# A channel mix placed behind the context's keys and values in the first attention unit of a fused RWKV and attention kernel

## The chip, the cores and the metric

The program runs on one core of one Trainium2 chip. The metric is the device time of one execution in microseconds (us), lower is better. The five engines used are TensorE (matmul), VectorE, ScalarE, GpSimd and SyncE, which here only issues DMA transfers.

## The reference, cut to what matters

Four layers run one after another on x (16 sequences of 128 tokens, 256 channels), all in float32: an RWKV mixer with a channel mix (L0), a cross-attention to a context (L1), a second RWKV mixer with channel mix (L2), a second cross-attention with an MLP (L3).

```python
x = _L0_xattn_ref(x, ctx_2048, ...)          # time mix, recurrence over the tokens, then channel mix
x = _L1_xattn_ref(x, ctx_2048, mask, ...)    # a = layer_norm(ctx); Q from x, K and V from a; x + tanh(gate) * out
x = _L2_xattn_ref(x, ctx_2048, 0, ...)
x = _L3_xattn_ref(x, ctx_2048, mask, ...)
```

What matters here: the K and V of L1 come from the layer norm of the context alone, and need nothing of x. The channel mix of L0 needs the x that the recurrence of L0 ends with:

```python
xc = _ln(x, ln2_w, ln2_b)                # channel mix
rr = sigmoid(xr2 @ fWr.T); kk = square(relu(xk2 @ fWk.T))
x = x + rr * (kk @ fWv.T)
```

## The kernel before, in words

The 16 sequences are worked on in four groups of four; 128 tokens lie on the partitions, or, after a transpose, 128 channels. For each layer pair and group there are two units: a *mixer* and an *attention unit*. STEPS lists eight of each (layers L0 and L1 of groups 0 to 3, then L2 and L3), four MLP units follow. The program of a mixer is written as two generators, `head` (H: norm, low-rank parts, projections of W, K, V, R, G) and `recurrence` (R: scans, outer products, the y sums, the output projection, x update). The channel mix of L0 is part of the attention unit of L1 (`attn`, A), since in the chain of units it comes just ahead of it; its semaphores have the prefix `f`.

Each engine runs its instructions strictly in the order in which they were emitted, and the order is written out by hand. A generator stops at each `yield`; the stretch between two yields is a step. ORDER (L103) has one string per engine, and `in_order` (L134) takes for each letter the next step of H, R or A:

```python
for letter in ORDER[engine]:
    next(programs[letter], None)
```

So a step can stand behind another one that waits on a semaphore, and is then held up by it, whatever its own inputs. VectorE has 595 such steps, ScalarE 540, TensorE 828, GpSimd 48.

The steps that the text speaks of, by their lines:

- Head, VectorE: five low-rank parts (`mix_low_rank`, L442), each a product in PSUM (L449) and a sum (L458), then the gate (L545). The parts make the inputs of W, K, V, R and G, in this order. TensorE: low-rank matmuls (L1184, the last ones L1198), w1 (L1223, L1228), projections of K, V and R (L1267), of G (L1281). ScalarE copies K, V, R out of PSUM (L892).
- Recurrence, VectorE: outer products (`outer`, L473), the reduction into RU (L556), for each of four chunks c two scans (L563) and a product with R_ (L571). An outer product for c of 2 or more waits until TensorE has summed the y of chunk c-2 (L1301). GpSimd makes YT = R * K * u (L780, L781), which the reduction into RU reads, and V * RU (L786). TensorE adds that in at L1291 and projects the output at L1129. VectorE adds it to x (L605).
- Attention unit of L1, in the emitted order of before: the bias split (L623, L626, first unit only); the channel mix: norm of x (L413, L421), transposes (L1079), shift (L439), two mixes (L432), key projection (L1088), two token projections (L1129), x update (L498, L499); then the norm of the context (mask work L636 to L641, L413, L421 into az), transposes of x (L1079 into QA) and of az (L1079 into QB), the Q projection (L1088 into QA), the K projection (L1088 into QB), the V projection (L1129 into QA); copies by ScalarE (L946, L993, L958, L975); then 16 score jobs.
- A norm takes VectorE's statistics, then GpSimd's power -0.5 (`inv_std`, L765: L767 and L768), then VectorE's application.
- A score job is a mask matmul (L1375) and two matmuls with the rows of Q spread out in QX (L1380). The spreading is done by DMAs (L386) that SyncE issues once both Q parts are written (L654); in SyncE's queue the load of the next mask row (L344) stands ahead of them. VectorE takes the maximum (L659), ScalarE the exponential (L1003), TensorE the transposes (L1393).

Buffers are shared. The channel mix of the attention unit uses az for its normed x, CT for its shifted copy, QA and QB in PSUM for its matmuls; the context's path uses az, CT, QA and QB too, and the same small buffers for its statistics.

The functions that the diff touches:

Of the kernel before, what the change touches and what calls it, by code (L numbers as in the profile page):

```python
# [14 lines left out]
HALF = C // P  # L15
# [84 lines left out]
for _group in range(G):  # L100
# [5 lines left out]
        "HHHHHHHHHHHHAHHRRHHRRRRRRRRRRRHRHHRRRHHRHHHRRRRHHRRAAHHAARRHAAHAAARARRHHARRAARRAARARRARAAHRAHAARAHRR"  # L106
        "HAAAHARRRARRHAHHAARARAAHHAAHHAAAHHRARAARRRRAARRAARARAHARAHRAAARRAARRRHAHAAHRHHRRHAARHHRAARHAHRAAAAAH"
        "HAAAHHRARHHRAARHHRHRAHHARAHRHAHARARARRRARAHHAARRRAAAAHHAARRRRARAHHRRARAAAARAAHHRRRRAAARAHHRHAARHHRRA"
        "RRRAARARRAAHRAHRRRRAHHARARRARAHHARRAAAAAHHRAARRAAARARRRAARRARAAHHARARRARRAHARHAARRHRAAHAHRRRRARAAHHR"
        "RRARAHHARRAAHHAARHHRRRRRRAAARRAARAARAARARAHHAARRHAHARAAAHRRRHHAAAARHHARRRAARAHHARRARHHRRRHRRRAAHRAAA"  # L110
        "RRARARAARARARARARARRARAAARRRAAAHHRARRRAHRHARHRARRARRAHHAHRRAAAAAAAHAAHAHAAAAAAAAAAAAAAAHHHAAAAH",
    "GpSimd":
        "HRRHAARRHAARRHAARHRARAHRRRARHRARAHRARARRHRAHAHHA",
    "ScalarE":
        "HHHHHHHHHHHRRRHHRRHRHRHHHHAHHAAAAHHRAAAAAAAAAAARAAAAHAAAAAARAAAAARAHARAAARAAHAARAAAAAHHHAHHAAAHHHAHR"
        "AAAAAAAARAAAAAAAAAAAAAAAAARHAAARRHARAHAARHAAHAAAAAAAHHHAAAHHHRAHAHAAAHAHAAAAARAAAAAHAAHAAARAAAAAHHHA"
        "AAARRARAHHARAAAAAAAAARHHAAAHAAAHRAAAHRAAAAARAAARARAAHHARHAAAAAHHAAAARAHHAAAARAARRAAAAAAHRHAAAAAAAAAA"
        "ARAAAAAHAAARAAAAAHRAARARAHRAAAAHHAAARAHAAHHAAARHRHRAAARHHAAAAAAAAAAARAAAAAAAHAAAAAAAARAAAHRRAHAAARAH"
        "AAAAARAAHHAHHARRAHHAAARRRAAHAHAAAAAAAAAAAAARAAAAAAARAAARAAARARAHAARAAAHAHHAAARRRARAAHAAHAAAAHAAAAAAA"
        "AAAAAAAAAAHAAAAAAHHAAAAAAAAAAAAHAHAAAAHA",  # L120
    "TensorE":
        "HHHHHHHHHHHHHHHHHHHHHHHRHRRRRRRHRRRRHRRRRRRHHHHHRHRHHRHHHHAHHAHAHAAAHHAAHHAHAHAAAAHRRARAAAARRAAHAAAA"
        "RRAAARARAAAAARRRRAAAAHAARRRRAAHHAAAAAHRHARRAHAAAHHHAHHAAHAHAAHHHHAHHAAAAAAAHRHRAARAAHRHAAAAARAAAARAA"
        "HRARAAAAAHRAAARRAARRRRRRHAAHHAHHARHAHAHAHARAAARAHAHAAHAHAAHHAHHHHAHHHHAHHAAAAHRARHHAHAHARAAARHAAAAAA"
        "RARHRARARHHARAAAARRAHHRAHAAHAARRRRAAHHAAHARHAARARAAAAHAHHHHHAAAAARRARHHAAAHRRAARARAHRHAARHRRRARAAHAA"
        "RRARRAAAHAAAHRHAHRRHAAAHAAHHRAAHHAAAARAAHARHAARRAARAHAHAAAAAHAAAHHAARHRAARRAAAAAHAAAARHARARRRRRAAAAR"
        "ARAAHARRRRAHAAAHARHHRRAAHAHAHAHARAHAHAHAAHRRRAHHRRHAHAAHHAAAAAAAAAHRHRARRAHAAAARHAARAAAAAAAHHARRARAA"
        "AAARRAARAAHAARRRRRHHAHAHAAHAAAHARARAHAHRAHHAHAHAHRAHRRARHAHRRAAAHAHAAAAAAAARRAAARRAAHAAAARAARARAHRHA"
        "ARAHRARRRAAAAARRRRAHAAHAARAARRHAHAHHRHHAAHARRRARAAAHAAARAHHAAHAHAHAAHAAAAAAAAAAAAAAAHAAAAAHAHAAAAAHH"
        "HAAAAAAAHAAAHAHAHHAHAAAAAAHH",  # L130
# [20 lines left out]
def build(nc, x, ctx, ctx_t, s0, state, mask_row, mask_col, rwkv_w, attn_w, mlp_w, bias_w, common, out):  # L151
# [5 lines left out]
    with ExitStack() as stack:  # L157
# [162 lines left out]
        with nc.Block() as block:  # L320
# [78 lines left out]
            def _(dve):  # L399
# [78 lines left out]
                def channel_mix(u, n, w, before):  # L478
# [131 lines left out]
                def attn(u):  # L610
# [18 lines left out]
                    if not mlp:  # L629
                        yield from channel_mix(u, "f", in_attn, 0)  # L630
                    yield
                    if not mlp:
                        dve.wait_ge(sem["ld_ctx"], 16 * (u.index + 1))
                        dve.wait_ge(lane_sem["ld_mask"][u.lane], 16)
                        dve.wait_ge(sem["ld_mrow"], 16 * (u.index + 1))
                        v.tensor_reduce(any_key[:], mrow8[:].rearrange("p (b s) -> p b s", b=NB), AX.X, ALU.max)\  # L636
                            .then_inc(sem["a_any"], 1)
                        v.tensor_copy(mcol[u.lane][:], mcol8[u.lane][:])
                    else:
                        dve.wait_ge(sem["ld_mrow"], 16 * (u.index + 1))  # L640
                    v.tensor_scalar(mrow[:], mrow8[:], 1.0, MASKED, ALU.subtract, ALU.mult).then_inc(sem["a_mask"], 1)  # L641
                    if mlp:
                        x_ready(u, 0)
                    norm_stats(src, abn, amv, sem["a_stats"])
                    yield
                    dve.wait_ge(sem["a_rstd"], u.at("a_rstd", 1))
                    norm_apply(az, src, amv, arstd, sem["a_z"])
# [165 lines left out]
            def _(act):  # L813
# [113 lines left out]
                def attn(u):  # L927
# [53 lines left out]
                    if not mlp:  # L981
                        yield from channel_mix(u, "f", in_attn)
# [593 lines left out]
```

## Time and profile before

| | |
|---|---|
| three runs | 1141.52, 1144.96, 1145.21 us; median 1144.96 |
| profiled execution, its own time | 1146.65 us |
| its span in the profile | 1144.7 us, 21376 instructions |
| mean granted TensorE clock | 0.966 of full speed |
| DMA | 24.80 MB, most of it in the first 30 us |

The span is the time from the first to the last instruction in the trace; the execution's own time is 1.95 us longer. A row of the timeline gives start and duration in us, engine, line, operation, the tile that is written and those that are read, their shapes, and how many instructions of a kind follow each other; in brackets stands how long the engine was idle before, and what released it. A float32 matmul of the program stands in the trace as two, so the four matmuls of a Q projection are "x8".

### The profile page before, as it was taken

How to read it: one execution, taken by the hardware profiler on the slowest of the kernel's cores; microseconds unless marked ns; L12 is line 12 of the kernel's file. 1: busy time of each engine (PE TensorE's matmuls, PEld its weight loads, DVE VectorE, ACT ScalarE, POOL GpSimd, SP SyncE). 2: the span in 40 equal slices, each digit the busy share in tenths (PEclk: the TensorE clock that was granted, in tenths of full speed). 3: DMA queues.
4: the chain of work that ended last, by engine and by line, in shares of the span. 5: the costliest groups of instructions: out<-in, count | busy, mean ns of one | idle time of the engine just before them, and what ended most of it. 6: DMA issues, size and time to landing. Idle time of an engine off the chain costs nothing. (4 is left out here: it accounts for less than half of the span.)

```text
span 1144.7 us, 21376 instructions
## 1 busy us (share of the span) xinstructions
PE 1032.4 (90%) x8866; PEld 774.9 (68%) x8866; DVE 780.4 (68%) x1078; ACT 536.1 (47%) x1643; POOL 109.5 (10%) x101
## 2 busy tenths in 40 slices
PE   7846889989998889978999989998999979999998
PEld 5634567766676657765667667785777757787777
DVE  3597759866996589779975688746986479532330
ACT  1102326743655235552476446642672445734762
POOL 1001010101010020002100202010100010000000
PEclk9967999989999899999999989999999989999999
DMA  9200000000000010000000000001000010000000
GB/s 371 87 0 1 2 25 16 1 2 20 21 2 2 1 32 10 1 2 19 17 6 2 20 20 2 2 2 41 9 1 2 11 38 3 1 1 21 27 10 19
DMA packets 17058, 24.80 MB, mean 22 GB/s; under 512 B 4417, under 2 KB 13761, under 8 KB 16322
## 3 DMA queue, kind: packets, MB, share of 16 engines
q1 hardware_dynamic: 16962, 23.44, 6.2%
q8 instruction: 70, 1.15, 0.4%
q14 instruction: 26, 0.21, 0.1%
HBM read 17.13 MB, written 2.10 MB: 17 GB/s over the span
## 5 line engine op out<-in xcount | busy, mean ns | idle before, releaser
L1003 ACT ACTIVATE big<-QB,nmax 128x128 f32<-128x128 f32 x512 | 181.6, 376 | 110.4 <-DVE nmax L659 109.2
L1301 PE MATMUL PB<-A,common_w 128*128 128x256 f32 x512 | 132.0, 399 | 21.7 <-DVE A L571 21.7
L563 DVE TENSOR_TENSOR_SCAN S_<-W_,A 128x1024 f32<-128x1024 f32 x64 | 146.5, 2311 | 0.3
L1380 PE MATMUL QB<-big,QX 128*128 128x256 f32 x512 | 135.7, 388 | 10.7 <-DMA QX<-big 10.7
L1301 PEld LDWEIGHTS PB<-A,common_w 128*128 128x128 f32 x512 | 97.8, 199 | 43.2 <-DVE A L571 26.7
L659 DVE TENSOR_REDUCE nmax<-QB 128x4 f32<-128x512 f32 x128 | 86.2, 683 | 54.0 <-PE QB L1380 52.7
L1380 PEld LDWEIGHTS QB<-big,QX 128*128 128x128 f32 x512 | 99.9, 196 | 30.3 <-DMA QX<-big 12.2
L1003 ACT ACTIVATION_READ_ACCUMULATOR big<-QB,nmax 128x1 f32 x512 | 110.2, 215 | 0.0
L1267 PE MATMUL PA<-X,rwkv_w 128*32 128x128 f32 x3072 | 100.9, 289 | 10.1 <-DVE X L458 9.8
L449 DVE SCALAR_TENSOR_TENSOR PA<-PA,rwkv_w,SX 128x512 f32<-128x512 f32 x80 | 56.5, 752 | 70.3 <-PE PA L1184 65.5
L1267 PEld LDWEIGHTS PA<-X,rwkv_w 128*32 128x32 f32 x3072 | 88.4, 117 | 22.3 <-DVE X L458 15.6
L1393 PE MATMUL QA<-common_w,big 128*128 128x128 f32 x512 | 78.6, 276 | 3.6 <-ACT CN L1012 2.2
L1393 PEld LDWEIGHTS QA<-common_w,big 128*128 128x128 f32 x512 | 60.8, 141 | 24.7 <-issue 16.3
L473 DVE TENSOR_TENSOR A<-K_,V_ 128x2032 f32<-128x2032 f32 x32 | 72.4, 2263 | 2.1 <-PE PB L1301 1.7
L571 DVE TENSOR_TENSOR A<-R_,S_ 128x2048 f32<-128x2048 f32 x32 | 73.2, 2287 | 0.6
L1375 PE MATMUL QB<-mrow,first_row 128*128 128x512 bf16 x128 | 49.8, 389 | 9.1 <-ACT big L1003 7.4
L1012 ACT ACTIVATE XT<-QA 128x512 f32<-128x512 f32 x64 | 38.7, 605 | 29.0 <-PE QA L1393 28.8
L458 DVE TENSOR_TENSOR X<-PA,XN 128x512 f32<-128x512 f32 x80 | 51.5, 685 | 1.2
L1184 PE MATMUL PA<-low,rwkv_w 32*128 32x256 f32 x256 | 44.8, 425 | 7.3 <-ACT K_ L892 1.9
L1129 PE MATMUL QA<-attn_w,CT 128*128 128x256 f32 x192 | 45.3, 382 | 4.5 <-DVE CT L678 4.5
L1012 ACT ACTIVATE CN<-QA 128x512 f32<-128x512 f32 x64 | 38.8, 606 | 20.1 <-PE QA L1393 19.8
L1129 PE MATMUL PB<-rwkv_w,S_ 128*128 128x256 f32 x192 | 45.4, 385 | 1.1 <-DVE S_ L598 1.0
(192 smaller groups left out, 1720.4 us busy)
## 6 DMA issues: line engine op xcount, KB each, us to landing
rwkv_w<-in_rwkv_w SPq DMA_DIRECT2D x2, 2866.0 KB, 14.9
QX<-big SPq DMA_DIRECT2D x128, 32.0 KB, 1.9
attn_w<-in_attn_w SPq DMA_DIRECT2D x2, 1031.5 KB, 17.2
mlp_w<-in_mlp_w SPq DMA_DIRECT2D x1, 2052.0 KB, 23.4
X<-in_x SPq DMA_DIRECT2D x4, 512.0 KB, 16.8
ctx<-in_ctx SPq DMA_DIRECT2D x4, 512.0 KB, 3.4
ctx<-in_ctx_t SPq DMA_DIRECT2D x4, 512.0 KB, 3.4
out<-XT SPq DMA_DIRECT2D x4, 256.0 KB, 2.0
```

What stands on the lines that cost most here:

```text
L449: last = v.scalar_tensor_tensor(pa4(h), pa4(h), r_pack[u.layer][:, col:col + 1], SX[:, h], ALU.add, ALU.mult)
L473: return v.tensor_tensor(A_[c % 2][:, :, :, 1:T], K_[:, :, 0:T - 1].unsqueeze(1).broadcast_to([P, DC, RS, T - 1]), V_[:, DC * c:DC * c + D ...
L563: last = v.tensor_tensor_scan(S_[:, d].rearrange("p k t -> p (k t)"), W_[:].rearrange("p k t -> p (k t)"), A_[c % 2][:, d].rearrange("p k ...
L571: v.tensor_tensor(A_[c % 2][:], R_[:].unsqueeze(1).broadcast_to([P, DC, RS, T]), S_[:], ALU.mult)\
L659: v.tensor_reduce(nmax[:, n % 2], bank(2 + n % 2).rearrange("p (j s) -> p j s", j=JH), AX.X, ALU.max, negate=True).then_inc(sem["a_max"], 1)
L1003: last = s.activation(PR[:, n % 2, j], bank(2 + n % 2)[:, j * T:(j + 1) * T], ACT.Exp, bias=nmax[:, n % 2, j:j + 1], accum_out=den[:, b, h ...
L1012: s.activation(PT[n % QUAD], bank(0).rearrange("p (j t) -> p j t", j=JH), ACT.Copy)\
L1129: last = t.matmul(dst[:, (b - base) * C:(b - base + 1) * C], lhs(h, b), w[:, h], start=(h == 0 and b == 2 * k), stop=(h == HALF - 1 and bi ...
L1267: last = t.matmul(PA[RH * b:RH * b + RH, k * T:(k + 1) * T], wt[:, h, RH * k:RH * k + RH], src[:, h, b * T:(b + 1) * T], start=(h == 0), s ...
L1301: last = t.matmul(y, ident, A_[c % 2][:, :, k], start=(c % 2 == 0 and k == 0), stop=False, skip_group_check=True)
L1380: last = t.matmul(o, QX[b % 2][:, i, h], K2[:, :, h, b * T:(b + 1) * T], start=False, stop=True, skip_group_check=True)
L1393: last = t.transpose(bank(0)[:, j * T:(j + 1) * T], PR[:, n % 2, j], ident)
```

## The change

In the first attention unit (`u.prior is None`) alone, the program is changed on four engines. The context's norm (VectorE), its reciprocal root (GpSimd), the copies of CT, K and V (ScalarE) and the transposes, K and V projections (TensorE) are emitted ahead of the channel mix instead of behind it. As the two share buffers, the channel mix gets new waits: VectorE waits for the transposes of az (`a_cT`) before it norms x into az, and for the V projection (`a_vp`) before it shifts into CT; TensorE waits for the copies of K and V out of QB and QA (`a_k`, `a_v`) before it transposes x into QA. The wait of the V projection for Q (`a_q`) falls away in this unit. The other attention units keep their order.

The ORDER strings of all four engines are new over their whole length, with the same number of each letter. On TensorE 422 of 828 steps stand at another position than before, on VectorE 298 of 595, on ScalarE 218 of 540, on GpSimd 6 of 48.

```diff
@@ VectorE
-                def channel_mix(u, n, w, before):
+                def channel_mix(u, n, w, before, free=lambda: None, shifted=lambda: None):
...
                     v.tensor_copy(CN[:, :, :, 0], st_sb[u.lane][:, 0])
+                    free()
                     norm_apply(w["z"], X, w["mv"], w["rstd"], sem[n + "_z"])
                     yield
+                    shifted()
                     shift(u, CS, CN, n + "_xn")
...
+                    def source_norm():
...
+                        norm_stats(src, abn, amv, sem["a_stats"])
+                        yield
+                        dve.wait_ge(sem["a_rstd"], u.at("a_rstd", 1))
+                        norm_apply(az, src, amv, arstd, sem["a_z"])
+
+                    if u.prior is None:
+                        yield from source_norm()
+                        yield from channel_mix(u, "f", in_attn, 0, lambda: dve.wait_ge(sem["a_cT"], u.at("a_cT", HALF)),
+                                               lambda: dve.wait_ge(sem["a_vp"], u.at("a_vp", 2)))
                     else:
...
+                        if not mlp:
+                            yield from channel_mix(u, "f", in_attn, 0)
+                        yield from source_norm()
@@ GpSimd
+                    norms = ["f", "a"] if u.kind == "attn" else ["a"]
+                    for n in norms[::-1] if u.prior is None else norms:
+                        yield
+                        pool.wait_ge(sem[n + "_stats"], u.at(n + "_stats", 1))
+                        inv_std(arstd[:], aveps[:], amv[:, :, 1], 1.0, NB, sem[n + "_rstd"])
@@ ScalarE
+                    def source():
                         yield
                         weights()
...
                         yield from keys_values()
+
+                    if u.prior is None:
+                        yield from source()
+                    if not mlp:
+                        yield from channel_mix(u, "f", in_attn)
+                    yield
+                    norm_x(0)
+                    if u.prior and not mlp:
+                        yield from source()
@@ TensorE
-                def channel_mix(u, n, w, free):
+                def channel_mix(u, n, w, free, room=None):
                     yield
+                    if room:
+                        room()
                     pe.wait_ge(sem[n + "_z"], u.at(n + "_z", 1))
...
                         if not mlp:
-                            pe.wait_ge(sem["a_q"], u.at("a_q", 2))
+                            if u.prior:
+                                pe.wait_ge(sem["a_q"], u.at("a_q", 2))
...
+                    def source():
+                        yield
+                        pe.wait_ge(sem["a_z"], u.at("a_z", 1))
+                        turn_tokens(lambda h: bank(2 + h), az, sem["a_cT"])
+                        if u.prior is None:
+                            pe.wait_ge(sem[f"ld_a{L}"], 16)
+                            yield from keys_values(CT[:])
+
+                    def source_read():
+                        pe.wait_ge(sem["a_k"], u.at("a_k", HALF))
+                        pe.wait_ge(sem["a_v"], u.at("a_v", 1))
+
+                    if u.prior is None:
+                        yield from source()
+                        yield from channel_mix(u, "f", in_attn, True, source_read)
```

The first letters of the strings, where the moved steps come in, read as steps:

- VectorE, before: second low-rank part, third, bias split, fourth, two outer products, fifth, RU, scans of chunk 0 and on. After: second, bias split, third, outer product 0, fourth, outer product 1, context statistics, context norm, RU, scans and product of chunk 0, scans of chunk 1, fifth part, product of chunk 1 and on. In the second mixer's head the fourth low-rank part comes wholly ahead of the x updates of the channel mix, and the fifth ahead of the first scan of the second recurrence instead of behind its second scan; the reduction into RU stays between the two Q parts.
- GpSimd, before: norm of head 0, YT, V * RU, norm of head 1, norm of the channel mix, norm of the context. After: norm of head 0, YT, norm of the context, V * RU, norm of head 1, norm of the channel mix.
- TensorE, after: the transposes and the K projection of the context come after the second of four L1198 steps of the first head, the projection of G a little later than before, the V projection ahead of the last quarter of the y sum of chunk 1; the w1 matmuls of the second head ahead of the last quarter of the y sum of chunk 3; between the Q projection and the first score three L1198 steps (before: two of them and K and V).

## Rows read from the trace of the kernel before

**Rows 1.** The page's busy time by engine, share of the span, instructions
```profile
PE 1032.4 (90%) x8866; PEld 774.9 (68%) x8866; DVE 780.4 (68%) x1078; ACT 536.1 (47%) x1643; POOL 109.5 (10%) x101
```
**Rows 2.** Busy time of each engine in two stretches, with its header
```profile
core 0: us, PE busy (x) PEld busy (x) DVE busy (x) ACT busy (x) POOL busy (x), PEclk, DMA share, GB/s
...
57.20:85.80 28.60, 14.01 (x44) 9.30 (x44) 26.12 (x15) 1.43 (x4) 2.50 (x2) 0.69 0.00 0
...
171.70:200.00 28.30, 27.00 (x155) 20.43 (x154) 27.26 (x23) 17.56 (x77) 0.00 (x0) 1.00 0.07 16
```
**Rows 3.** Timeline of TensorE, 69 to 107 us
```profile
69.04 2.08 PE L1301 MATMUL PB<-A,common_w 128*128 128x256 f32 x4 [11.38 <-DVE A L571]
...
86.69 5.49 PE L1301 MATMUL PB<-A,common_w 128*128 128x256 f32 x12 [4.10 <-DVE A L571]
...
102.21 3.72 PE L1301 MATMUL PB<-A,common_w 128*128 128x256 f32 x16 [1.39 <-DVE A L571]
105.77 1.89 PE L1223 MATMUL PA<-X,rwkv_w 128*128 128x256 f32 x8
```
**Rows 4.** Timeline of TensorE, 146 to 175 us
```profile
146.69 3.62 PE L1129 MATMUL QB<-rwkv_w,big 128*128 128x256 f32 x16
152.49 0.43 PE L1267 MATMUL PA<-X,rwkv_w 128*32 128x128 f32 x8 [2.18 <-DVE X L458]
153.08 5.15 PE L1267 MATMUL PA<-X,rwkv_w 128*32 128x128 f32 x120 [0.17 <-DVE X L458]
...
159.09 1.04 PE L1079 MATMUL QB<-common_w,az 128*128 128x128 f32 x8
...
162.04 3.70 PE L1088 MATMUL QA<-XT,attn_w 128*128 128x512 f32 x8
...
166.09 3.70 PE L1088 MATMUL QB<-CT,attn_w 128*128 128x512 f32 x8
...
170.14 3.72 PE L1129 MATMUL QA<-attn_w,CT 128*128 128x256 f32 x16
...
173.91 1.03 PE L1380 MATMUL QB<-big,QX 128*128 128x256 f32 x4
```
**Rows 5.** Timeline of VectorE, 39 to 80 us
```profile
39.71 1.42 DVE L449 SCALAR_TENSOR_TENSOR PA<-PA,rwkv_w,SX 128x512 f32<-128x512 f32 x2 [6.30 <-PE PA L1184]
...
57.76 1.42 DVE L449 SCALAR_TENSOR_TENSOR PA<-PA,rwkv_w,SX 128x512 f32<-128x512 f32 x2 [2.17 <-PE PA L1198]
...
60.42 1.86 DVE L556 TENSOR_REDUCE RU<-YT 128x128 f32<-128x1024 f32 x1
...
77.53 2.28 DVE L473 TENSOR_TENSOR A<-K_,V_ 128x2032 f32<-128x2032 f32 x1 [1.71 <-PE PB L1301]
```
**Rows 6.** Timeline of VectorE, 153 to 178 us
```profile
153.94 1.40 DVE L413 BATCH_NORM_STATS2 abn<-ctx 128x6 f32<-128x256 f32 x4
...
157.16 1.39 DVE L421 TENSOR_SCALAR az<-ctx,amv,arstd 128x256 f32<-128x256 f32 x4 [1.41 <-POOL arstd L768]
...
165.36 1.91 DVE L556 TENSOR_REDUCE RU<-YT 128x128 f32<-128x1024 f32 x1 [0.55 <-POOL YT L781]
167.18 0.75 DVE L654 TENSOR_SCALAR big<-QA,attn_w 128x512 f32<-128x512 f32 x1
...
175.60 2.28 DVE L571 TENSOR_TENSOR A<-R_,S_ 128x2048 f32<-128x2048 f32 x1
```
**Rows 7.** Timeline of GpSimd: the end of YT, and the context's reciprocal root
```profile
57.88 1.90 POOL L781 TENSOR_TENSOR YT<-YT,rwkv_w 128x1024 f32<-128x1024 f32 x1
...
156.12 1.01 POOL L768 TENSOR_TENSOR arstd<-aveps,half_pow 128x4 f32<-128x4 f32 x1
```
**Rows 8.** Busy time and granted clock in one stretch, columns as in rows 2
```profile
153.00:156.00 3.00, 2.92 (x64) 2.92 (x68) 2.72 (x12) 0.00 (x0) 0.16 (x1) 0.59 0.03 5
```
**Rows 9.** Timeline of SyncE's queue in a layer-1 unit
```profile
659.58 0.33 SPq L344 DMA_DIRECT2D mrow<-in_mask_row  x1
```
**Rows 10.** Timeline of TensorE in the same unit
```profile
663.75 2.08 PE L1380 MATMUL QB<-big,QX 128*128 128x256 f32 x4 [3.75 <-DMA QX<-big]
```
**Rows 11.** Timeline of TensorE: first and last of 14 gaps over 1 us
```profile
241.67 1.99 PE L1129 MATMUL QA<-attn_w,CT 128*128 128x256 f32 x8 [1.48 <-DVE CT L678]
...
934.48 0.39 PE L1375 MATMUL QB<-mrow,first_row 128*128 128x512 bf16 x1 [1.16 <-ACT big L1003]
```

More of the change, by code:

```diff
@@ L105 @@
     "VectorE":
[L106 to L110, printed above, removed]
@@ L627, in attn @@
                             dve.wait_ge(sem["bias_setup"], steps)
[L629 to L638, printed above, removed]
-                    else:
-                        dve.wait_ge(sem["ld_mrow"], 16 * (u.index + 1))
@@ L641, in attn @@
[L641 to L647, printed above, removed]
+                    def source_norm():
+                        yield
+                        if not mlp:
+                            dve.wait_ge(sem["ld_ctx"], 16 * (u.index + 1))
+                            dve.wait_ge(lane_sem["ld_mask"][u.lane], 16)
+                            dve.wait_ge(sem["ld_mrow"], 16 * (u.index + 1))
+                            v.tensor_reduce(any_key[:], mrow8[:].rearrange("p (b s) -> p b s", b=NB), AX.X, ALU.max)\
+                                .then_inc(sem["a_any"], 1)
+                            v.tensor_copy(mcol[u.lane][:], mcol8[u.lane][:])
+                        else:
+                            dve.wait_ge(sem["ld_mrow"], 16 * (u.index + 1))
+                        v.tensor_scalar(mrow[:], mrow8[:], 1.0, MASKED, ALU.subtract, ALU.mult).then_inc(sem["a_mask"], 1)
+                        if mlp:
+                            x_ready(u, 0)
+                        norm_stats(src, abn, amv, sem["a_stats"])
+                        yield
+                        dve.wait_ge(sem["a_rstd"], u.at("a_rstd", 1))
+                        norm_apply(az, src, amv, arstd, sem["a_z"])
@@ L979, in attn @@
                         yield from keys_values()
-                    if not mlp:
-                        yield from channel_mix(u, "f", in_attn)
-                    yield
-                    norm_x(0)
-                    if not mlp:
+                    def source():
                         yield
@@ L1339, in attn @@
                         yield from keys_values(ctx_chan)
-                    if not mlp:
+                    def source():
[11 more added lines that the diff above has]
+                        yield from channel_mix(u, "f", in_attn, True, source_read)
+                    elif not mlp:
                         yield from channel_mix(u, "f", in_attn, True)
@@ L1351, in attn @@
                         turn_tokens(bank, X2[u.lane], sem["a_xT"])
-                        yield
-                        pe.wait_ge(sem["a_z"], u.at("a_z", 1))
-                        turn_tokens(lambda h: bank(2 + h), az, sem["a_cT"])
+                        if u.prior:
+                            yield from source()
                     yield
@@ L1358, in attn @@
                     chan_proj(QA, ah_(L, "Wq"), XT, sem["a_qp"], lambda h: pe.wait_ge(sem["a_xc"], u.at("a_xc", h + 1)))
-                    if not mlp:
+                    if u.prior and not mlp:
                         yield from keys_values(CT[:])
```

46 lines of the change are left out of this document (23 added, 23 removed).

## The prediction

> **What bounds the kernel now.** I began with busy time by engine [rows 1]: TensorE is busy for 90% of the span, VectorE for 68%, so work taken off TensorE's queue counts in full wherever TensorE is the bound. Then the stretches [rows 2]: from 57 to 86 us TensorE works 14.0 of 28.6 us at a mean granted clock of 0.69, while VectorE works 26.1. There the recurrence of the first mixer (scans and outer products) is the bound. From 172 to 200 us both are full (27.0 and 27.3 of 28.3). The order of TensorE's work [rows 3] shows the holes: 11.38 us before 69.0, 4.10 before 86.7. The change puts the context's transposes, keys and values there. What has to be asked is what that costs VectorE in the same stretch, and what those projections covered where they stood.
>
> **The change part by part.**
> *TensorE's load.* Context transposes (1.04 us), Q projection (3.70), K projection (3.70), V projection (3.72) stand between 159.1 and 173.9 [rows 4]. The first, third and fourth, 8.5 us, leave this place for the holes. In the holes they cost TensorE nothing: K needs some 5 us from 66 on (partly at half clock), and the scans need TensorE next at about 72; V goes in where VectorE is the slower by 10 us. The 8.5 us is the gross gain.
>
> *The bias split* on VectorE goes ahead of the third low-rank part, into a wait of 6.30 us [rows 5]: nothing. The first outer product goes ahead of the fourth part and has to wait for the last half of V_: 0.6 us late, taken from the wait of 2.17 us before the fifth [rows 5].
>
> *The context's norm* on VectorE costs 1.0 us of mask work and 1.8 of statistics, then 1.4 to apply [rows 6]. New place: right after the second outer product, at about 54.0. Statistics end at 56.8. The reciprocal root (about 1.4 us with its hand-over [rows 7]) comes from GpSimd, whose new order has it behind the R*K product, and this ends at 59.8 now [rows 7], 60.4 with the 0.6 above. So az is normed from 61.8 to 63.2: VectorE waits 5 us with everything queued behind, the scans included. The reduction into RU starts at 63.2, not 60.4 [rows 5]: +2.8. Then the fifth low-rank part (2.7 us), which stood ahead of that reduction, comes after the second pair of scans; it takes the place of a wait of 1.71 [rows 5]: +1.0. The recurrence is a chain of VectorE work from there on, so +3.8.
>
> *Order at the end of the first recurrence.* One w1 matmul group (1.89 us [rows 3]) goes ahead of the last quarter of the last y sum. What it delays by 1.9 also brings the next low-rank tanh earlier; I take +0.3, bounds 0 and 1.9. So the first x update ends at 131.3, +4.1.
>
> *Channel mix of unit 0.* Its new waits (for az turned, for V read, for K and V out of PSUM) hit things finished some 10 to 40 us earlier; only ScalarE's copy of V stands shortly before, and it runs beside VectorE's norm: nothing. With +4.1 the last V matmuls end at 154.4 (150.3 now [rows 4]). The fourth low-rank part is now wholly ahead of the x updates, so TensorE no longer waits 2.18 us before the R projection and the clock doesn't fall for it: 3.9 us for what took 7.9 from the end of V, wait included [rows 4]. That wait is what brought the clock to 0.59 in the three us behind it [rows 8]. R ends at 158.3, now 158.2: the delay is made good.
>
> *From there to the first score.* X is turned, XT copied, Q projected: from about 161.6, now 162.0. VectorE's second Q part stays behind the reduction into RU [rows 6] and ends at 167.0, now 167.9. Now K and V run while Q goes through the spreading DMAs. In the new order nothing but 1.5 us of low-rank matmuls is left between Q and the first score. How long that is, the layer-1 units show: the mask row's DMA is issued at 659.58 [rows 9], right after Q, and the first score matmul starts at 663.75 after 3.75 us idle [rows 10]. So 4.2 us: first score at 171.2, now 173.9. **Gain 2.7**, with 4 us idle in place of 7.4 us of work. And the next four matmuls take 2.08 us where 1.03 is usual [rows 10, 4], the following score pair the same: 1 to 2 us back. VectorE, meanwhile, does the fifth low-rank part before the scans instead of after; its first product with R_ ends about 178.7, now 177.9 [rows 6].
>
> The Trainium skill (TensorE: Matmul & The Clock Gate, HAM oscillation) says that an engine which waits between short bursts re-throttles and begins each burst at half rate. Here the trace agrees for the 3.75 us wait. By it the new wait costs what I charge; without it the forecast would be 1 to 2 us lower.
>
> *Everything later.* 422 of TensorE's 828 steps stand a few places off (counted in the two order strings), with the same instructions. No row prices that. Idle gaps over 1 us after 171.7 are 14, 27.8 us in all, from 1.48 to 1.16 us for the first and last [rows 11]. Closing a quarter of them would give -7, opening as many +7; I take 0, since the same work meets the same bound.
>
> **Sum.** -8.5 for K, V and transposes, -4.0 for the R projection, +4.1 for the recurrence, +4.0 idle before the score, and +1.7 of small waits and of the Q part behind RU make -2.7; +1.2 for the clock leaves -1.5. Against the profiled execution (1146.65, span 1144.7) that is 1145.2; it lies 1.7 above the median of the three runs, so the median comes to 1143.5.
>
> **The rivals.**
> *The gain stays (1137.5).* If the softmax chain and TensorE's queue are what counts after 171 us, and the 4 us of waiting for Q's DMA is taken by work that had no place (or the later order closes some 5 us of the gaps), what remains is 8.5 + 4.0 - 4.1 - about 1 = 7.4. For it: TensorE is 90 to 98% busy later, and it has 8.5 us less in its queue for good. Against it: in this order nothing independent stands between Q and the scores.
> *Slower, by the clock in the recurrence (1150).* In the new order TensorE waits about 2 us for the fifth low-rank part (76.3 to 78.2) and again before the last y sum. A wait of 2.18 us did bring the clock down [rows 4, 8]; one of 1.39 before 102.2 did not [rows 3]. If both do, V's 3.72 us becomes 7.4 in front of the matmuls that release the last outer product (0.7 of slack, so +2.9), and the last 16 y matmuls take 7.3 instead of 3.7 (12 took 5.49 at half clock, 16 took 3.72 at full [rows 3]): +3.6. With -1.5 that is +5.0. It decides once more than 4.9 of these 6.5 us come about. For it: such stretches exist now; against it: those bursts are longer than the waits.
> *It does nothing visible:* my own case.
>
> **How the numbers follow.** Forecast (between -3.4 and +3.4 of the median) 0.39, gain stays 0.37, slower 0.24. The measurement tells about 0.3%, 3.4 us, from no change. These are the chances of same, faster and slower. For the range, the gain case spans 1134.5 to 1141 and the slower one 1148.4 to 1153; 1136 to 1151 leaves out about a tenth at each end.
>
> **What would show it.** Right: TensorE's hole at 57 to 69 us holds L1079 to QB and L1088 to QB; VectorE waits some 5 us for arstd before az near 62; the last outer product of the first recurrence starts near 91.6 (87.8 now); no wait before the R projection near 154; 3 to 4 us idle on QX before the first score, at about 171, at half clock after it. Wrong: if az is normed before 60 or the first x update ends before 129 (then the gain stays); if V runs at half clock before 90 (then slower); if the first score starts before 168; or if the difference at 180 us and that at the end differ by over 3 us, which would put the cause in the later orders.

## The result and the profile after

| | before | after |
|---|---|---|
| median of the runs | 1144.52 us (22 runs, 1141.12 to 1146.73) | 1141.15 us (22 runs, 1137.96 to 1144.23) |
| ratio | | **0.9969**, interval 0.9960 to 0.9977 |
| profiled execution, its own time | 1146.65 us | 1137.96 us |
| span, mean granted clock | 1144.7 us, 0.966 | 1136.1 us, 0.973 |

The changed kernel is faster by 0.31%, 3.4 us; the interval, 2.6 to 4.6 us, lies clear of no change. The two profiles differ by 8.6 us, since one shows an execution of before near its slowest and the other the fastest of after. So times deep in the two traces can't be subtracted. In the first 180 us differences of 1 to 2 us can be the execution's as well; experiments 1 and 2 show by how much.

Busy time by engine on the page of after. VectorE, ScalarE and GpSimd are busy a little less, TensorE 6.5 us less than in [rows 1] with the same 8866 matmuls. The granted clock, 0.973 for 0.966, goes the same way.

```profile
PE 1025.9 (90%) x8866; PEld 771.6 (68%) x8866; DVE 778.7 (69%) x1078; ACT 533.8 (47%) x1643; POOL 104.5 (9%) x101
```

Busy time in the stretches of [rows 2, 8], columns as there.

```profile
57.20:85.80 28.60, 18.67 (x65) 11.54 (x66) 24.59 (x18) 2.97 (x5) 3.52 (x4) 0.88 0.05 18
153.00:156.00 3.00, 3.00 (x85) 2.62 (x87) 2.93 (x6) 0.04 (x1) 0.00 (x0) 1.00 0.02 5
171.70:200.00 28.30, 27.28 (x145) 20.02 (x144) 27.06 (x20) 15.22 (x69) 0.00 (x0) 0.93 0.06 12
```

From 57 to 86 us TensorE now works 18.7 us where it had 14.0. In the last stretch it is just as full as before, but at a clock of 0.93 it gets through ten matmuls fewer. The reason is in its timeline.

TensorE after, from the first recurrence to the scores; lines L1301, L1267 and L1380 of before are L1316, L1282 and L1410 here, and the K and V projections are L1101 and L1142.

```profile
64.51 4.62 PE L1101 MATMUL QB<-CT,attn_w 128*128 128x512 f32 x8
...
84.87 3.62 PE L1142 MATMUL QA<-attn_w,CT 128*128 128x256 f32 x16
...
105.09 2.86 PE L1316 MATMUL PB<-A,common_w 128*128 128x256 f32 x12 [1.32 <-DVE A L573]
...
150.22 3.72 PE L1142 MATMUL QB<-rwkv_w,big 128*128 128x256 f32 x16
153.88 3.70 PE L1282 MATMUL PA<-X,rwkv_w 128*32 128x128 f32 x128
...
170.59 2.08 PE L1410 MATMUL QB<-big,QX 128*128 128x256 f32 x4 [4.60 <-DMA QX<-big]
...
172.88 1.92 PE L1410 MATMUL QB<-big,QX 128*128 128x256 f32 x4
174.59 2.41 PE L1296 MATMUL PA<-X,rwkv_w 128*128 128x512 f32 x4
```

K and V stand in the holes, partly at half clock for K and at full clock for V. The R projection starts with no wait and takes 3.70 us. The first score comes at 170.6, against 173.9 in [rows 4], but TensorE has waited 4.60 us on Q's DMAs for it, and this score and the next run at half speed, the gate projection behind them in part (2.41 us for 1.88).

VectorE after, the rows that answer to [rows 5, 6].

```profile
54.23 1.40 DVE L413 BATCH_NORM_STATS2 abn<-ctx 128x6 f32<-128x256 f32 x4
...
61.00 1.38 DVE L421 TENSOR_SCALAR az<-ctx,amv,arstd 128x256 f32<-128x256 f32 x4 [4.97 <-POOL arstd L778]
62.30 1.92 DVE L558 TENSOR_REDUCE RU<-YT 128x128 f32<-128x1024 f32 x1
...
90.72 2.27 DVE L473 TENSOR_TENSOR A<-K_,V_ 128x2032 f32<-128x2032 f32 x1
...
130.86 1.41 DVE L413 BATCH_NORM_STATS2 abn<-X 128x6 f32<-128x256 f32 x4
...
172.70 0.69 DVE L669 TENSOR_REDUCE nmax<-QB 128x4 f32<-128x512 f32 x1 [2.23 <-PE QB L1410]
175.62 2.29 DVE L573 TENSOR_TENSOR A<-R_,S_ 128x2048 f32<-128x2048 f32 x1
```

The context's norm waits 4.97 us for the reciprocal root behind YT on GpSimd, and everything behind it is late: RU by 1.9 us against [rows 5], and two more steps against these rows of VectorE before:

```profile
87.81 2.27 DVE L473 TENSOR_TENSOR A<-K_,V_ 128x2032 f32<-128x2032 f32 x1
...
127.22 1.40 DVE L413 BATCH_NORM_STATS2 abn<-X 128x6 f32<-128x256 f32 x4
```

The last outer product is 2.9 us late, the statistics of the first channel mix 3.6. By the end of the first product with R_ both kernels stand at 177.9, against [rows 6]. So 8.5 us of TensorE's work were moved into holes, and on VectorE's path nothing had come of it by there in these two traces. Then where do 3.4 us come from?

### The profile page after: what moved, and what is told of

Its sections match the earlier page's. It is cut to its first block, busy times and chain, and to the rows that moved or that the text cites. A ratio compares the mean times of both kernels' runs of the same rounds, so it can differ in the third digit from the quotient of the medians.

```text
span 1136.1 us, 21377 instructions
## 1 busy us (share of the span) xinstructions
PE 1025.9 (90%) x8866; PEld 771.6 (68%) x8866; DVE 778.7 (69%) x1078; ACT 533.8 (47%) x1643; POOL 104.5 (9%) x101
## 4 chain that ended last, share of the span: by engine, by line
PE 65%; DVE 19%; ACT 8%; issue 4%; POOL 2%; DMA 1%; SPq 1%; DVEq 0%; ACTq 0%; POOLq 0%
PE PA L1282 7%; PE QB L1410 6%; PE PB L1316 6%; PE QA L1142 5%; PE PB L1142 5%; DVE S_ L565 5%; PE PA L1199 3%; PE QA L1423 3%; PE QB L1101 3%; ACT big L1016 3%; DVE A L573 3%; PE PA L1122 2%; PE QA L1132 2%; PE QA L1434 2%; PE PA L1132 2%
## 5 line engine op out<-in xcount | busy, mean ns | idle before, releaser
L1410 PE MATMUL QB<-big,QX 128*128 128x256 f32 x512 | 137.8, 394 | 15.5 <-DMA QX<-big 15.5
L1316 PE MATMUL PB<-A,common_w 128*128 128x256 f32 x512 | 124.3, 384 | 6.1 <-DVE A L573 6.1
L1410 PEld LDWEIGHTS QB<-big,QX 128*128 128x128 f32 x512 | 101.2, 199 | 34.7 <-DMA QX<-big 17.1
L1316 PEld LDWEIGHTS PB<-A,common_w 128*128 128x128 f32 x512 | 95.0, 191 | 28.7 <-DVE A L573 10.8
L1282 PE MATMUL PA<-X,rwkv_w 128*32 128x128 f32 x3072 | 95.7, 281 | 8.0 <-DVE X L458 7.9
L1282 PEld LDWEIGHTS PA<-X,rwkv_w 128*32 128x32 f32 x3072 | 84.5, 113 | 18.5 <-DVE X L458 11.5
L1142 PE MATMUL QA<-attn_w,CT 128*128 128x256 f32 x192 | 45.0, 381 | 3.0 <-DVE CT L688 3.0
L1142 PE MATMUL PB<-rwkv_w,S_ 128*128 128x256 f32 x192 | 45.4, 385 | 0.2
## 6 DMA issues: line engine op xcount, KB each, us to landing
mlp_w<-in_mlp_w SPq DMA_DIRECT2D x1, 2052.0 KB, 23.6
```

The source lines that it names most:

```text
L1142: last = t.matmul(dst[:, (b - base) * C:(b - base + 1) * C], lhs(h, b), w[:, h], start=(h == 0 and b == 2 * k), stop=(h == HALF - 1 and bi ...
L1282: last = t.matmul(PA[RH * b:RH * b + RH, k * T:(k + 1) * T], wt[:, h, RH * k:RH * k + RH], src[:, h, b * T:(b + 1) * T], start=(h == 0), s ...
L1316: last = t.matmul(y, ident, A_[c % 2][:, :, k], start=(c % 2 == 0 and k == 0), stop=False, skip_group_check=True)
L1410: last = t.matmul(o, QX[b % 2][:, i, h], K2[:, :, h, b * T:(b + 1) * T], start=False, stop=True, skip_group_check=True)
```

## The experiments

Each ratio is to before, timed beside it, with its 95% interval. Each experiment has 4 to 12 executions and before 17 or more beside them, in three series with medians of before of 1144.15, 1143.83 and 1144.23 us. A trace shows one execution only. The change has two parts that can be parted: the program of one unit, and order strings that are new over their whole length. The strings have the same number of each letter up to certain places, where one kernel's can be joined to the other's. The first cut lies near 280 us, the second near 655 us.

### 1 and 2. The early part alone, the later orders alone

```diff
 early_new (after's program)          late_new (before's program)
-ORDER = after[:]                    -ORDER = before[:]
+ORDER = after[:cut] + before[cut:]  +ORDER = before[:cut] + after[cut:]
 cut: VectorE 139, GpSimd 12, ScalarE 104, TensorE 173 steps
```

> The changed kernel with the four order strings of before from the second attention unit's first score on: only the moved steps and the new order of the first 170 us or so are left of the change. Theory (what is gained is gained early, by taking K, V and the transposes out of TensorE's full stretch): ratio to before about 0.9975, a gain of 2.5 to 3 us, first score near 170.6. Rival (the early part is even, the whole gain comes from the later orders): ratio 0.999 to 1.001.

> The kernel before with the new order strings from the second attention unit's first score on, nothing moved in the first unit. Theory (gain is early): ratio 0.999 to 1.000, under 1 us. Rival (gain is in the later orders): about 0.997, 3 to 4 us. If both parts add, this ratio times that of early_new is about 0.997, the change's own.

Measured: early_new 1144.56 us, ratio **1.0002** (0.9988 to 1.0017); late_new 1139.96 us, ratio **0.9961** (0.9948 to 0.9974). The product, 0.9963, is the whole change within its interval. All of the gain that can be told comes from orders in which no K, V or transpose of the first unit has moved.

late_new holds a second lesson. Up to 280 us it is instruction for instruction the kernel before. Its timeline of TensorE:

```profile
151.49 0.42 PE L1267 MATMUL PA<-X,rwkv_w 128*32 128x128 f32 x8 [2.18 <-DVE X L458]
152.09 3.48 PE L1267 MATMUL PA<-X,rwkv_w 128*32 128x128 f32 x120 [0.17 <-DVE X L458]
...
171.50 1.03 PE L1380 MATMUL QB<-big,QX 128*128 128x256 f32 x4
```

The same wait of 2.18 us stands ahead of the R projection as in [rows 4], and there 5.15 us followed at half clock, here 3.48 at full. The first score comes at 171.5, where before's profile has it at 173.9. So 2.4 us of the apparent gain at that point is the difference between two executions of one code. The Trainium skill (TensorE: Matmul & The Clock Gate, Part 1: The HAM clock gate) says that the number of matmuls that run at the lower clock differs between runs of one kernel; these two rows agree for a clock that falls, too.

The later experiments add to this. Eight of the traces (before and seven others) run before's code up to 280 us, and four (after, early_new, clock_kept, gate_in_hole) run after's up to the first score. Of the eight, six run the R projection at full clock behind that same wait, and two at half (before, and late_mid_kept with 5.15 us). The times of one step spread by 2 us and more within one code:

| step | before's code, eight traces | after's code | forecast of the difference |
|---|---|---|---|
| last outer product starts | 86.0 to 88.3, mean 87.1 | 90.7, 91.1, 91.3, 90.7; mean 90.9 | +3.8 |
| statistics of the first channel mix | 126.2 to 128.2, mean 127.0 | 130.9, 132.5, 133.0, 130.6; mean 131.7 | +4.1 |
| first score starts | 171.5 to 173.9, mean 172.6 | after 170.6, early_new 171.5 | -2.7 |
| first product with R_ ends | 175.5 to 177.9, mean 176.6 | after 177.9, early_new 178.9 | +0.8 |

So the two profiles of the last section understated the delay of the recurrence (3.8 us, not 2.9) and overstated the lead of the first score. At the first product with R_ the changed early part is not even but 1.3 and 2.3 us behind the mean of the eight: before's profile had the latest of them.

### 3. Half of the new wait filled with the gate projection

The first half of the second mixer's gate projection goes ahead of the first score, on TensorE alone.

```diff
 TensorE, after's step order around the first score of unit 0
+H1 gate projection, first half
 A0 mask row and first score
 A0 second score
-H1 gate projection, first half
```

> The changed kernel, but the first half of the gate projection (1.9 to 2.4 us on TensorE) stands ahead of the first score in place of behind the second, so that it fills part of the 4.6 us in which TensorE waits for QX. Its input is ready at 168.2, the scores' at 170.6. Theory (that wait is paid in full by the end, since TensorE is the bound after it): first score still near 170.6, the steps behind it 2 us earlier, ratio to before about 0.9955, 1.5 to 2 us better than the changed kernel. Rival (VectorE is the bound at 170 to 200 us, and the wait costs nothing): the same as the changed kernel, 0.997.

Measured: 1141.57 us, ratio **0.9975** (0.9963 to 0.9988), no better than the change. TensorE's timeline of it:

```profile
168.87 3.78 PE L1296 MATMUL PA<-X,rwkv_w 128*128 128x512 f32 x4 [2.23 <-DVE X L458]
...
172.87 1.91 PE L1410 MATMUL QB<-big,QX 128*128 128x256 f32 x4
```

The gate's input is ready only 2.23 us into the wait. The projection then takes 3.78 us where it takes 1.9 at full clock. From the end of the L1213 steps to the first score it is 6.2 us here, 5.1 in after, so the score is pushed back by 1.1 us. (The two traces have it 2.3 us apart, but 1.2 of these were there before the wait.) Once the two scores and the gate projection are done, TensorE is 2 us ahead of after. But VectorE waits for the first score: it stands idle for 3.21 us ahead of its maximum, 2.23 in after, its first product with R_ ends 1.0 us later, counted from the same L1213 steps, and TensorE then waits 1.73 us for that product. So what TensorE won, VectorE's wait for the score took.

### 4. The fifth low-rank part in the norm's wait

```diff
 VectorE                             TensorE
 A0 context statistics               H0 first two L1213 steps of the last part
+H0 fifth low-rank part (L449, L458) +H0 last two L1213 steps
 A0 context norm                     A0 transposes, K projection of the context
 RU, scans, product of chunk 0       ...
 scans of chunk 1                    -H0 last two L1213 steps
-H0 fifth low-rank part
```

> The changed kernel, but the first head's fifth low-rank part (2.7 us on VectorE) stands between the context's statistics and its norm, in the 5 us in which VectorE waits for the reciprocal root, and on TensorE the last two L1213 steps stand ahead of the context's transposes. Theory (the delay of the first recurrence, +2.9 at its third outer product, is on the path and reaches the first score): that outer product at 77.8 in place of 80.4, first x update and first score 2.6 us earlier (168.0), ratio about 0.995. Rival (slack behind the recurrence takes it up): the outer product is earlier, the end is not, 0.997.

Measured: 1139.85 us, ratio **0.9957** (0.9941 to 0.9973). VectorE's timeline of it:

```profile
59.54 1.42 DVE L449 SCALAR_TENSOR_TENSOR PA<-PA,rwkv_w,SX 128x512 f32<-128x512 f32 x2 [1.56 <-PE PA L1213]
60.99 1.29 DVE L458 TENSOR_TENSOR X<-PA,XN 128x512 f32<-128x512 f32 x2
62.96 1.38 DVE L421 TENSOR_SCALAR az<-ctx,amv,arstd 128x256 f32<-128x256 f32 x4 [0.68 <-POOL arstd L778]
```

The wait of 4.97 us became 1.56 and 0.68 with 2.7 us of needed work between them. From outer product 1 to outer product 2 it is 26.9 us, 29.5 in after. But in this trace the lead was gone by the first score, which had been expected 2.6 us earlier: from outer product 1 to the score it is 119.7 us here and in after. On the way the last y sum's 12 matmuls took 4.50 us after a wait of 2.32, 2.86 in after. That is no mark of this experiment: early_new (4.29) and clock_kept (4.54), with after's code up to there, show it too. The ratio is better than the change's, but the intervals overlap, so whether the delay of the recurrence is paid at the end stays open here.

### 5 and 6. Which of the later orders

Before's program, with after's strings between the two cuts alone (VectorE's steps 139 to 357, GpSimd's 12 to 27, ScalarE's 104 to 295, TensorE's 173 to 464), or behind the second alone.

```diff
+late_mid:  before[:cut1] + after[cut1:cut2] + before[cut2:]
+late_end:  before[:cut2] + after[cut2:]
```

> The kernel before, nothing moved in the first unit, with the new order strings only between the second attention unit's first score and the first layer-1 unit's (about 280 to 655 us). The kernel before with all later orders new gave 0.9961. The traces put the first layer-1 unit's norm 1 to 3 us earlier from this stretch, clock apart. Theory (the middle is where the new orders gain): ratio about 0.997 to 0.9975. Rival (the last 490 us gain): 0.9995 to 1.0005.

> The kernel before with the new order strings only from the first layer-1 unit's first score (about 655 us) on. From that unit's norm to the end both kernels with the new orders take about the same as the two with the old ones in the traces (before 496.2, early_new 494.5, changed 495.2, late_new 494.5 us). Theory: ratio 0.999 to 1.0. Rival: 0.997. The product of this ratio and that of late_mid should be about 0.996.

Measured: late_mid 1138.03 us, ratio **0.9951** (0.9936 to 0.9965); late_end 1144.9 us, ratio **1.0006** (0.9996 to 1.0016). The gain lies between 280 and 655 us. Busy time from the context's statistics in unit 1 to the norm of the first layer-1 attention unit, columns as in [rows 2], first in before:

```profile
272.50:645.30 372.80, 340.26 (x3247) 250.52 (x3238) 291.66 (x390) 187.35 (x590) 42.52 (x29) 0.98 0.04 10
```

In late_end, where this stretch is unchanged:

```profile
271.40:644.00 372.60, 340.22 (x3247) 250.54 (x3239) 291.57 (x391) 187.12 (x590) 42.44 (x29) 0.98 0.04 10
```

In late_mid:

```profile
270.90:638.40 367.50, 336.67 (x3247) 249.09 (x3240) 290.38 (x390) 186.63 (x590) 40.08 (x29) 0.99 0.04 10
```

In the whole change:

```profile
268.50:637.70 369.20, 338.81 (x3248) 250.96 (x3240) 288.65 (x390) 186.64 (x590) 39.53 (x29) 0.98 0.04 10
```

The two kernels with the old order need 372.6 and 372.8 us here, the two with the new one 367.5 and 369.2 (early_new 371.2, late_new 367.6). Between before and late_mid the same 3247 matmuls take 3.6 us less, and TensorE's idle time falls by 1.7 (32.5 to 30.8). Here the traces hardly spread: before, late_end and before_kept need 372.6 to 372.8 us, the four kernels with before's start and the new middle 367.5 to 367.6. Cut at VectorE's norm statistics, the stretch shows where the 5.3 us between before and late_mid lie (TensorE's busy time and granted clock behind each length):

| from, to in before's trace | before | late_mid | difference |
|---|---|---|---|
| 272 to 337 | 64.3; 59.7 at 1.00 | 64.6; 60.0 at 1.00 | +0.3 |
| 337 to 371 | 34.6; 30.3 at 1.00 | 33.3; 29.5 at 1.00 | -1.2 |
| 371 to 397 | 25.5; 21.9 at 0.87 | 24.2; 20.6 at 0.93 | -1.3 |
| 397 to 420 | 23.6; 20.8 at 0.93 | 22.3; 19.7 at 1.00 | -1.3 |
| 420 to 506 | 85.5; 80.4 at 1.00 | 85.5; 80.5 at 1.00 | 0.0 |
| 506 to 645 | 139.5; 127.1 at 0.98 | 137.7; 126.4 at 0.98 | -1.8 |

In two of the pieces the clock rises, and there the busy time falls by 2.4 us together. The rest, 2.9 us, is 1.7 of idle time and 1.2 of busy time at an unchanged clock. And the piece from 371 to 397 is no sure gain: early_new, with the old order, needs 24.2 us there, and after, with the new one, 25.3. Nothing was taken out of TensorE's work.

### 7. The new wait filled with throwaway matmuls

The kernel has a function `keep_clock`, which multiplies the identity into a bank of PSUM that the next real matmul overwrites. One call after the mask row's wait in the first score fills the wait for Q's DMAs. The added matmuls compute nothing that is used, here and in all experiments below whose name says kept.

```diff
 # TensorE, scores(), ahead of the first score; unit 0
+keep_clock(bank(2)[:, 0:P], {0: 14}.get(u.index, 0))
```

> The changed kernel with 14 matmuls of the identity into a free PSUM bank (about 4 us of work whose result is overwritten) in the wait for QX ahead of the first score, so that TensorE doesn't stand still there. First score still near 170.6, at full clock: 1.03 us for the four in place of 2.08, and the next score pair and the gate projection faster, 2 to 2.5 us on TensorE's queue by 177. Theory (the clock after that wait is on the path): ratio to before about 0.9955, 1 to 2 us under the changed kernel. Rival (VectorE is late anyway at that point, its first product with R_ ends at 177.9 whatever TensorE does): the same as the changed kernel, 0.997.

Measured: 1139.68 us, ratio **0.9961** (0.9947 to 0.9975). TensorE's timeline of it:

```profile
169.21 3.36 PE L1178 MATMUL QB<-common_w 128*128 128x128 f32 x28
...
173.84 1.13 PE L1411 MATMUL QB<-big,QX 128*128 128x256 f32 x4 [1.05 <-DMA QX<-big]
```

The clock stays up: 1.13 us for four matmuls that took 2.08. The score starts at 173.8 and not near 170.6 as expected, but this execution was late already (its R projection starts 3.6 us after that of after); from the end of the L1213 steps to the score it is 4.7 us, 5.1 in after. TensorE then waits 1.4 us for VectorE's first product with R_ instead, so little arrives at the end; the intervals don't part this kernel from after.

### 8 and 10. The same in three layer-1 units, with and without the new orders

```diff
 # before's program; late_clock_kept has late_new's strings, before_kept before's own
+keep_clock(bank(2)[:, 0:P], {4: 12, 5: 6, 6: 12}.get(u.index, 0))
```

> The kernel with nothing moved and the later orders new, plus 12, 6 and 12 identity matmuls in the waits for QX of three layer-1 units (3.75, 2.5 and 3.8 us of idle). Theory (the half clock behind two of these waits costs 2 to 3 us each, and is paid in the end): ratio about 0.992 to 0.994. Rival (the softmax chain or VectorE takes it up): 0.996, as without them.

> The kernel before with 12, 6 and 12 identity matmuls in the waits for QX of three layer-1 units, no step moved. With all later orders new, the same fill gave 0.9934 against 0.9961 without. Theory: the half clock behind these waits costs some 3 us in all orders alike, ratio about 0.9973. Rival (it was the order's luck): 1.0000.

Measured: late_clock_kept 1136.49 us, ratio **0.9934** (0.9919 to 0.9949), against 0.9961 without the fills; before_kept 1139.29 us, ratio **0.9953** (0.9941 to 0.9965). TensorE's timeline of before_kept, where [rows 10] had 3.75 us idle and then 2.08 for the score:

```profile
657.39 2.94 PE L1163 MATMUL QB<-common_w 128*128 128x128 f32 x24 [0.36 <-DVE big L654]
...
661.53 1.13 PE L1381 MATMUL QB<-big,QX 128*128 128x256 f32 x4 [0.98 <-DMA QX<-big]
```

Thirty matmuls that compute nothing, with not one step moved, bring at least as much as the whole change: 5.3 us (4.0 to 6.8), against 3.4 (2.6 to 4.6). Without them only two of the three waits end in a score at half clock in before (663.75 and 927.16); behind the third, of 2.32 us at 797.25, the four matmuls took 1.13 us anyway.

### 9. One move out of the middle

At 402 us in before, the R projection of mixer 3 runs at half clock behind a wait of 2.23 us. Of the middle's moves one alone is made here: the transposes of x of attention unit 2 come after the low-rank matmuls of mixer 3's R part.

```diff
 # TensorE
-"...HAAHAHAAHHAHHHHAHHHHAHHAAAAHRA..."
+"...HAAHAHAAHHHHAHHAHHHHAHHAAAAHRA..."
```

> The kernel before with one step of TensorE's order moved: in the third attention unit the transposes of x (1.09 us) stand behind the two low-rank matmuls of the R projection instead of ahead of them, as in the new orders. In the trace of before TensorE waits 2.23 us ahead of that R projection and runs it at half clock (5.55 us at 402.4); with the new orders it waits 1.21 and takes 3.9. Theory (a good part of what the new orders gain is this kind of wait, cut short enough for the clock to stay): 1.7 to 1.9 us, ratio about 0.9984. Rival (the gain is spread over many small moves, this one is nothing): 1.0000.

Measured: 1143.0 us, ratio **0.9986** (0.9977 to 0.9995). TensorE's timeline, first of before:

```profile
402.44 5.55 PE L1267 MATMUL PA<-X,rwkv_w 128*32 128x128 f32 x128 [2.23 <-DVE X L458]
```

and of x_turn_later:

```profile
399.55 0.42 PE L1267 MATMUL PA<-X,rwkv_w 128*32 128x128 f32 x8 [1.21 <-DVE X L458]
400.14 3.48 PE L1267 MATMUL PA<-X,rwkv_w 128*32 128x128 f32 x120 [0.17 <-DVE X L458]
```

In the old place 1.09 us of transposes stood ahead of what VectorE needed for R's input. In the new one VectorE is released earlier, TensorE waits 1.21 us instead of 2.23, and 128 matmuls take 4.1 us with their pause instead of 5.55. The R projection ends 1.7 us earlier, counted from the start of the stretch. At the end of the stretch 0.8 is left of it (371.9 us against 372.7), since from 506 to 645 us this trace needs 0.4 more, at a clock of 0.96 for 0.98. late_mid shows the same wait of 1.21 at 398.45. This place is no matter of chance in the traces: with the old order the projection runs at half clock in all four that have it (before, late_end, before_kept, early_new), with the new one in none.

### 11 and 12. The parts joined

```diff
+late_mid_kept: late_mid and keep_clock with {4: 12, 5: 6, 6: 12}
+all_kept:      after, fifth_in_wait's order, and keep_clock with {0: 14, 4: 12, 5: 6, 6: 12}
```

> The new orders in the middle stretch alone (0.9951) with the same fill. If the two add: 0.9925, the best so far, some 4 to 5 us under the changed kernel, with nothing moved in the first attention unit.

> The changed kernel with the fifth low-rank part in VectorE's wait (0.9957 alone) and the fill in all four waits for QX, the first unit's too (0.9961 alone for that one). Theory (the early part, mended, is worth a little over before's): 0.992, the same as late_mid_kept or 0.5 us under it. Rival (the early part stays even, whatever is mended there): 0.9935, as late_clock_kept.

Measured: late_mid_kept 1134.8 us, ratio **0.9915** (0.9902 to 0.9927), where 0.9951 times 0.9953 is 0.9904: the gains of order and of fills stand beside each other. all_kept 1131.52 us (1128.42 to 1136.63), ratio **0.9892** (0.9872 to 0.9913), span 1130.8 us at a clock of 0.980: faster than before by 12.4 us and than after by some 9. VectorE's timeline of all_kept:

```profile
61.84 1.38 DVE L421 TENSOR_SCALAR az<-ctx,amv,arstd 128x256 f32<-128x256 f32 x4 [0.69 <-POOL arstd L778]
...
88.91 2.27 DVE L473 TENSOR_TENSOR A<-K_,V_ 128x2032 f32<-128x2032 f32 x1
...
128.83 1.40 DVE L413 BATCH_NORM_STATS2 abn<-X 128x6 f32<-128x256 f32 x4
...
174.22 2.29 DVE L573 TENSOR_TENSOR A<-R_,S_ 128x2048 f32<-128x2048 f32 x1
```

and of TensorE:

```profile
170.12 1.13 PE L1411 MATMUL QB<-big,QX 128*128 128x256 f32 x4 [1.62 <-DMA QX<-big]
171.09 0.38 PE L1406 MATMUL QB<-mrow,first_row 128*128 128x512 bf16 x1
171.31 1.03 PE L1411 MATMUL QB<-big,QX 128*128 128x256 f32 x4
```

The first product with R_ ends at 176.5, 1.4 us earlier than in before's and after's profiles, with the last outer product of the first recurrence 1.8 us earlier than in after. Against the mean of the eight traces with before's early code, 176.6, that is even: with its two mends the early part no longer loses anything by there. At the norm of the first layer-1 unit all_kept stands at 635.6 us, the eight other traces with the new middle at 637.5 to 640.4, so the moved K and V may gain something in the end; one trace, and executions from 1128 to 1137 us, don't show it. The single parts give 0.9969 (after) times 0.9988 (the fifth part) times 0.9992 (the fill in unit 0) times 0.9953 (the other fills), 0.9902 together, inside the interval of all_kept. With the 0.9973 that the same fills gave on late_new's order it is 0.9922, just above it. How much each of the two mends is worth beside the others, and the same kernel with before's orders behind 655 us, was not tried.

## Why the prediction was right and wrong

The forecast was -1.5 us with a chance of 0.39 for no visible change; the measured -3.4 lies between it and the gain that stays, right at the border of 3.4 us beyond which "faster" had 0.37. The range held the time, in part by luck: the gain came from a term that the sum took as nothing. The prediction had named the sign for this, a difference at 180 us and one at the end over 3 us apart, and it came in: 177.9 against 177.9 in the profiles, 3.4 us at the end.

**Right, in the first attention unit.** Nearly every place in after's trace came in as worked out, within 1 to 1.5 us:

| step | forecast | trace of after |
|---|---|---|
| wait for the reciprocal root | 5 us | 4.97 |
| az normed | 61.8 to 63.2 | 61.0 to 62.4 |
| last outer product | near 91.6 | 90.7 |
| first x update late by | 4.1 | 3.6 (at the statistics that follow it; 4.7 by the means) |
| wait before the R projection | none | none |
| last part of Q written (L664) | 167.0 | 165.5 |
| first score | 171.2, 4.2 behind it | 170.6, 5.1 behind it |
| idle for Q's DMAs, score behind it | 4 us, half clock | 4.60 us, 2.08 us |
| first product with R_ ends | 178.7 | 177.9 |

The first score is right by two misses that cancel: Q was ready 1.5 us earlier than forecast, and its DMAs took 0.9 us longer. early_new measures the sum by itself: 1.0002, with an interval from -1.4 to +1.9 us; the forecast's -1.5 lies at its edge, so the early part is even or nearly so.

**Mis-sized: the clock in the -4.0 of the R projection.** 1.7 of these 4.0 us were the half clock of [rows 4, 8]. Six of the eight traces of this code, late_new among them, have the same wait without it. So I charged the gain of one execution as if every execution had it to win; the term is 2.2 in six and 4.0 in two. With 1.7 less the sum is +0.2 us, and early_new measured +0.2; so close a match is chance, given its interval of 3.3 us.

**A count that was wrong.** After 171.7 us before's trace has 17 gaps over 1 us on TensorE, 34.8 us in all, where the prediction and [rows 11] have 14 and 27.8. A quarter of them is 8.7 us; the reason for taking 0 didn't rest on it.

**The rival that it is slower by the clock in the recurrence** came in by half, in some executions. A wait of 2.35 us for the fifth part did arise ahead of the gate projection at 77.66, but its four matmuls took 1.98 us, and V at 84.87 took 3.62, at full clock. At the last y sum, the rival's other place, 12 matmuls took 2.86 us in after and gate_in_hole, but 4.29 in early_new and 4.54 in clock_kept, with the same code up to there: 1.4 to 1.7 us more, where the rival had 3.6.

**The step that failed: "Everything later … I take 0, since the same work meets the same bound."** Measured, it is -4.5 us (late_new), of which the middle has all (late_mid, -5.6) and the end none (late_end, +0.7 with 0 in its interval). The same work didn't meet the same bound. Of the middle's 5.3 us by the traces, 1.7 is idle time that went, 2.4 is busy time in pieces where the clock rose, which the reason given left out, and some 1.2 is busy time at an unchanged clock, whose cause is open. The bounds of 7 us either way held it. I could have looked for waits near 2 us followed by doubled durations, as in [rows 4], all along the trace of before and asked which of them the new strings remove. x_turn_later is one such, 1.6 us by its ratio (0.6 to 2.6), 0.8 by its trace at 640 us. For the rest the pieces are known (337 to 371, 371 to 397 and 506 to 645 us) but not the moves; that stays open.

**The gain stays** was also half right, for the reason in its brackets alone: the later order brought some 5 us, though only 1.7 of them as closed gaps. The reason that it stood on, TensorE's lighter queue after 171 us, did not show in early_new (1.0002).

## What to carry to other kernels

A block that is moved into a hole also leaves one where it stood: ask what it covered there (here Q's DMAs, 4.6 us and then half clock), and fill both before judging the move. Where a change comes with a rewritten order, time the two apart by joining the strings; here they gave 1.0002 and 0.9961, and the second had nothing to do with the idea of the change. Kernels that share their first part repeat its measurement: here eight traces of one code had the first score at 171.5 to 173.9 us, so take the mean of such traces before a step of 1 or 2 us is credited to a change. Where TensorE must wait some 4 us for a DMA on its critical path, throwaway matmuls sized to end just ahead of it are worth trying first, since they move nothing.

## What was not expected of the hardware

- One code, eight executions: behind a wait of 2.18 us the granted clock was 0.59 over three us in before, and the 120 matmuls took 5.15 us there and in late_mid_kept, 3.48 in the six others. Behind 2.23 us at 402 us it fell in all four traces that have this wait, and behind 2.17 to 2.53 us at the second layer-1 unit's first score the four matmuls took 1.13 to 1.19 us, at full clock, in all ten traces without a fill there. So the length of a wait alone doesn't say whether the clock falls. That such differences make up the spread, with the profiled executions of before and after 8.6 us apart where the medians are 3.4 apart, is my reading; the cause of the spread was not measured by itself.
- Fills in three waits gave 5.3 us in before (0.9953), where 3.1 had been expected from units such as [rows 10]. With late_new's order the same fills gave 0.9934 against 0.9961, some 3 us. From the norm of the first layer-1 unit to the end of the trace, the only part in which these fills stand, the ten traces without them need 497.7 to 499.6 us and the four with them 494.1 to 496.4, 3.4 less on the mean. That fits the 3.1; the rest of the 5.3 lies within its interval.
